# A four-block transformer kernel: the feed-forward with constants made earlier, statistics in three pieces, a new order of steps, and sums moved to TensorE

## The chip, the cores and the metric

The program runs on one core of a Trainium2 chip. A core has five engines that run their own instruction streams and meet at semaphores: TensorE (PE in the profile), VectorE (DVE), ScalarE (ACT), GpSimd (POOL) and SyncE (SP, which starts the transfers here). The metric is the device time of one execution in microseconds (us); lower is better.

## The reference, cut to what matters

The input x has 16 sequences of 256 tokens with 128 features. Four blocks follow each other, each as x + block(layernorm(x)): attention A (16 heads of 64, causal), the feed-forward, attention B (16 heads of 8), and the same feed-forward again. The change is in the feed-forward:

```python
h = gelu(concat(x, slot_mean) @ w1 + b1)
route_logits = (h @ w2 + b2) / (abs(tau) + 0.1)          # 64 slots per token
topk_vals, topk_idx = top_k(route_logits, 8)
alpha = (one_hot(topk_idx, 64) * softmax(topk_vals)[..., None]).sum(axis=-2)
si = einsum('bts,btd->bsd', alpha, x) / (alpha.sum(axis=1) + 1e-08)[..., None]
gi = si @ Wih.T + bih;  gh = S @ Whh.T + bhh             # S: the slots, the same for all
r = sigmoid(i_r + h_r);  z = sigmoid(i_z + h_z);  n = tanh(i_n + r * h_n)
S_new = (1.0 - z) * n + z * S
q = S_new @ wq + bq;  k = S_new @ wk + bk;  v = S_new @ wv + bv
y = S_new + softmax(q k^T * scale) @ v
y = (y - mean(y)) * rsqrt(var(y) + 1e-05) * ln_g + ln_b
out = einsum('bts,bsd->btd', alpha, y @ wvp + bvp) @ wo + bo
```

## The kernel before, in words

The residual X stays on chip as 32 tiles of 128 tokens by 128 features. The four blocks follow one another on every engine. Each block is written once per engine as a function `do` that says what this engine does in a step of a given kind; lists of steps (A_PLAN, B_PLAN, F_PLAN) give the order, the same list for all engines. An engine takes its steps strictly in that order and waits at semaphores (`f["..."]`, `a_...`, `b_...`), so a step late in the list can't start before an earlier one of the same engine.

*Attention A* works on one sequence and a group of four heads at a time; its last steps are in the last call of a_steps (lines 68 to 97) and in A_EPILOGUE (line 142), the drain: the last weighted sums (`pv`), their division (`normal`, DVE writes a_o), the transposes (`turn`), the projection (`project`: 16 products of 128 columns) and the addition to X on DVE. *Attention B* runs two sequences per trip; its drain is B_EPILOGUE (line 149). There POOL multiplies (line 891), DVE reduces (`gather`, line 858), POOL divides, the result goes through memory and back, PE transposes and projects it (`finish`, line 763), and ACT writes X.

*The feed-forward* treats the 32 tiles as two chunks of 16 (c = 0, 1). Its steps by name:
- `stats` and `apply`: the mean and variance of each token (bn_stats, bn_aggr on DVE), 1/sqrt by a power on POOL (norm_rstd, line 371), and the normalised tile f_xs on DVE (norm_apply, line 375). Chunk 0 has them as ffn_stats and ffn_apply in the drain of the attention ahead (lines 98 and 99, and B_EPILOGUE).
- `hidden`, `logits`: transposes of f_xs, a product with w1 and Gelu on ACT, a product with w2 (lines 917 to 939).
- `top`: DVE's max8 of 64 logits, the difference to the largest, and match_replace, which marks the eight taken (lines 1083 to 1096). `alpha`: exp on ACT, then on DVE the masked exp, its sum over 64, the reciprocal and the product (lines 1097 to 1104).
- `read`: PE sums the tokens of each slot and transposes alpha; ACT copies the transposes. `slots`, `inputs`: DVE divides (f_si, line 1115), PE transposes, ACT copies f_sit, PE multiplies by wih in three products of 512 columns (line 957).
- `gates`, `candidate`, `new`: DVE adds gate_h to two of them (line 1121), ACT's tanh, and the new slots f_sn. `qkv`, `scores`, `probs`, `attend`: the small attention among slots.
- `ynorm`: DVE subtracts y's mean and multiplies by 1/sqrt, PE transposes. `values`: the product with wcomb (ln_g, wvp and wo in one) and the addition of crow. `out`: 16 products with alpha, and DVE's addition to X in four pieces.

The order is `hidden`, `apply`, `logits` for both chunks, then `top 0`, `alpha 0`, `read 0`, `top 1`, `slots 0` and so on; from `gates` on, chunk 1 runs two steps behind chunk 0. gate_h, wcomb, crow and the other constants come from set_tensor and set_vector (lines 1200 to 1240), which run between attention A and the first feed-forward.

PSUM has eight banks. Each chunk of the feed-forward uses four (f_banks); the first transposes take banks 0 and 1, which attention A's projection also uses, so `hidden` 0 waits until all of X has been added.

## Time and profile before

| | |
|---|---|
| median of 3 runs | 945.12 us (944.6 to 946.56) |
| the profiled execution | 945.51 us, its span 943.7 us |
| mean granted TensorE clock | 0.922 |
| busy | PE 84%, DVE 71%, ACT 51%, POOL 43% of the span |
| attention A | to about 518 us |
| first feed-forward, with its constants | to about 615 us |
| attention B | to about 837 us |
| second feed-forward, with B's drain | to the end |

Times in the trace count from the span's start. A line of the timeline gives the start, the time from it to the end of the last instruction that it merges, the engine, the line of the kernel, the operation, what it writes and reads, and how many instructions; in brackets how long the engine had been idle and what ended that. The granted clock is a share of TensorE's full 2.4 GHz; it takes two levels, 0.5 and 1, so a value between is a mean over time.

### The profile page before, as it was taken

How to read it: one execution, taken by the hardware profiler on the slowest of the kernel's cores; microseconds unless marked ns; L12 is line 12 of the kernel's file. 1: busy time of each engine (PE TensorE's matmuls, PEld its weight loads, DVE VectorE, ACT ScalarE, POOL GpSimd, SP SyncE). 2: the span in 40 equal slices, each digit the busy share in tenths (PEclk: the TensorE clock that was granted, in tenths of full speed). 3: DMA queues.
4: the chain of work that ended last, by engine and by line, in shares of the span. 5: the costliest groups of instructions: out<-in, count | busy, mean ns of one | idle time of the engine just before them, and what ended most of it. 6: DMA issues, size and time to landing. Idle time of an engine off the chain costs nothing.

```text
span 943.7 us, 25617 instructions
## 1 busy us (share of the span) xinstructions
PE 789.8 (84%) x10324; PEld 606.5 (64%) x10324; DVE 672.3 (71%) x1528; ACT 480.2 (51%) x849; POOL 409.8 (43%) x302
## 2 busy tenths in 40 slices
PE   1899999999999999999986876667888888839655
PEld 0688888888888888888875553534555555525435
DVE  3767667776677766677674776536999999966773
ACT  1678766787767777677752423013444433315220
POOL 1454444544445444454442100116888888751000
PEclk9999999999999999999996778768999999958786
DMA  6000000000000000000000000000221111120002
GB/s 274 1 3 1 0 0 0 0 0 0 0 0 0 0 0 0 0 0 0 1 1 2 0 1 1 1 0 1 23 24 22 22 22 22 20 27 1 1 1 89
DMA packets 71588, 13.25 MB, mean 14 GB/s; under 512 B 66432, under 2 KB 70528, under 8 KB 70912
## 3 DMA queue, kind: packets, MB, share of 16 engines
q1 hardware_dynamic: 71552, 12.76, 6.2%
q8 instruction: 24, 0.39, 0.2%
q14 instruction: 12, 0.10, 0.0%
HBM read 8.56 MB, written 4.19 MB: 14 GB/s over the span
## 4 chain that ended last, share of the span: by engine, by line
PE 63%; DVE 19%; ACT 8%; issue 5%; POOL 3%; DMA 1%; DVEq 0%; ACTq 0%; SPq 0%; POOLq 0%
PE PS L533 6%; PE PS L490 6%; PE PS L349 5%; PE PS L350 4%; PE PS L351 4%; PE PS L426 3%; PE PS L732 3%; DVE b_prod L843 3%; PE PS L722 3%; PE PS L526 2%; PE PS L512 2%; PE PS L724 2%; PE PS L1015 2%; DVE a_nm L607 2%; PE PS L497 2%
## 5 line engine op out<-in xcount | busy, mean ns | idle before, releaser
L640 POOL TENSOR_TENSOR a_pl<-a_p,a_ph 128x1024 f16<-128x1024 f32 (+1 forms) x128 | 210.7, 1646 | 256.3 <-ACT a_ph L562 256.3
L891 POOL TENSOR_TENSOR b_w<-b_v,b_e 128x2048 f32<-128x2048 f32 x32 | 137.8, 4307 | 13.9 <-ACT b_e L811 13.9
L559 ACT ACTIVATE a_p<-PS 128x1024 f32<-128x1024 f32 (+1 forms) x128 | 103.7, 810 | 74.8 <-PE PS L497 74.7
L607 DVE TENSOR_REDUCE a_nm<-PS 128x4 bf16<-128x512 f32 (+1 forms) x128 | 121.5, 949 | 0.0
L843 DVE TENSOR_TENSOR b_prod<-PS,b_qt 128x512 f32<-128x512 f32 x128 | 85.4, 682 | 26.3 <-PE PS L724 22.0
L562 ACT ACTIVATE a_ph<-PS 128x1024 f16<-128x1024 f32 (+1 forms) x128 | 103.1, 805 | 0.0
L552 ACT ACTIVATE a_qk_h<-PS 128x512 f16<-128x512 f32 x128 | 73.4, 604 | 57.1 <-PE PS L351 55.8
L372 POOL TENSOR_TENSOR veps<-mv,eps 128x2 f32<-128x2 f32 (+2 forms) x40 | 8.0, 201 | 190.4 <-DVE mv L1165 136.9
L596 DVE TENSOR_TENSOR a_qk_l<-PS,a_qk_h 128x512 f16<-128x512 f32 x128 | 87.0, 681 | 3.4 <-ACT a_qk_h L552 3.4
L512 PE MATMUL PS<-a_vh,a_ph 128*128 128x65 f16 x768 | 78.5, 196 | 0.3 <-issue 0.3
L514 PE MATMUL PS<-a_vl,a_ph 128*128 128x64 f16 x768 | 78.3, 194 | 0.0
L516 PE MATMUL PS<-a_vh,a_pl 128*128 128x65 f16 x768 | 78.0, 195 | 0.0
L349 PE MATMUL PS<-xhl,a_wqk_h 128*128 128x256 f16 x256 | 70.8, 277 | 8.5 <-ACT xhl L550 7.5
L512 PEld LDWEIGHTS PS<-a_vh,a_ph 128*128 128x128 f16 x768 | 70.5, 98 | 11.1 <-issue 9.5
L858 DVE TENSOR_REDUCE b_s<-b_w 128x128 f32<-128x2048 f32 x32 | 72.8, 2277 | 4.9 <-POOL b_w L891 4.9
L722 PE MATMUL PS<-b_kh,w_rolls 128*128 128x256 f16 x256 | 65.9, 285 | 11.4 <-DVE b_prod L843 8.0
L603 DVE TENSOR_TENSOR a_vl<-PS,a_vh 128x512 f16<-128x512 f32 x64 | 44.3, 692 | 41.8 <-ACT a_vh L555 41.8
L514 PEld LDWEIGHTS PS<-a_vl,a_ph 128*128 128x128 f16 x768 | 71.4, 100 | 0.1
L516 PEld LDWEIGHTS PS<-a_vh,a_pl 128*128 128x128 f16 x768 | 71.4, 98 | 0.0
L351 PE MATMUL PS<-xhl,a_wqk_l 128*128 128x256 f16 x256 | 70.4, 275 | 0.0
L350 PE MATMUL PS<-xhl,a_wqk_h 128*128 128x256 f16 x256 | 70.3, 275 | 0.0
L724 PE MATMUL PS<-b_kl,w_rolls 128*128 128x256 f16 x256 | 65.3, 283 | 0.0
(225 smaller groups left out, 2038.7 us busy)
## 6 DMA issues: line engine op xcount, KB each, us to landing
scratch_dram<-b_o SPq DMA_DIRECT2D x32, 64.0 KB, 3.6
b_y<-scratch_dram SPq DMA_DIRECT2D x16, 128.0 KB, 2.1
out_dram<-X SPq DMA_DIRECT2D x2, 1024.0 KB, 3.9
w_rest<-rest_dram SPq DMA_DIRECT2D x1, 1862.0 KB, 15.2
X<-x_dram SPq DMA_DIRECT2D x1, 1792.0 KB, 11.2
w_first<-first_dram SPq DMA_DIRECT2D x1, 1600.0 KB, 7.1
w_rolls<-rolls_dram SPq DMA_DIRECT2D x1, 544.0 KB, 15.8
X<-x_dram SPq DMA_DIRECT2D x1, 256.0 KB, 3.6
```

The costliest lines, as they stand in the source:

```text
L349: pe.matmul(dst, ah, bh, start=start, stop=False, skip_group_check=True)
L350: pe.matmul(dst, ah, bl, start=False, stop=False, skip_group_check=True)
L351: return pe.matmul(dst, al, bh, start=False, stop=stop, skip_group_check=True)
L512: pe.matmul(O[q][:, h * W:(h + 1) * W], ph[:, nx, par, pair, at], a_vh[:, (g - 1) % GA, k, h, :], start=first, stop=False, skip_group_chec ...
L514: pe.matmul(O[q][:, h * W:h * W + EA], ph[:, nx, par, pair, at], a_vl[:, (g - 1) % GA, k, h, :], start=False, stop=False, skip_group_check ...
L516: ins = pe.matmul(O[q][:, h * W:(h + 1) * W], pl[:, nx, par, pair, at], a_vh[:, (g - 1) % GA, k, h, :], start=False, stop=h == 3 and k == ...
L559: act.activation((a_p0, a_p1)[j][:, me, :, :, :].rearrange("p a h q -> p a (h q)"), TT[:, :, 0:512 - 256 * j], ACT.Exp, scale=EA ** -0.5)
L562: act.activation((a_ph0, a_ph1)[j][:, me, :, :, :].rearrange("p a h q -> p a (h q)"), TT[:, :, 0:512 - 256 * j], ACT.Exp, scale=EA ** -0.5 ...
L607: dve.tensor_reduce(a_nm[:, nx, j, :].rearrange("p (a h) -> p a h", a=2)[:, :, 0:2], MM[:, :, 0:256 * (j + 1)].rearrange("p a (h k) -> p a ...
L640: pool.tensor_tensor(*(n[:, g % 2, :, :, :].rearrange("p a h q -> p (a h q)") for n in (pl, p, ph)), ALU.subtract).then_inc(a_split, 1)
L843: dve.tensor_tensor(b_prod[:, j, :, :], T[j % 2][:, :].rearrange("p (e t) -> p e t", e=2), b_qt[:, 1 - par, :].unsqueeze(1).to_broadcast([ ...
L891: pool.tensor_tensor(b_w8[:, j, :, :, :], rolled_values(par, j, 0, H), rolled_exps(par, j, 0, H), ALU.mult).then_inc(b_weighed, 1)
```

## The change: what it does

1. *Constants in the drain of A.* set_tensor and set_vector are split in two parts. Part 0 stands at the end of the last group of heads, ahead of ffn_apply; part 1 in A_EPILOGUE behind the last `normal`. All their sums now lie in two banks, S1 and S2.
2. *Statistics in three pieces* (PIECES): tiles 0 to 15, 16 to 27, 28 to 31. In the drain of A the second piece goes ahead of the last projection; in B the first piece moves into the last trip, ahead of a `gather`, and the second into B_EPILOGUE. Only four tiles are left for the feed-forward itself. `hidden` 0 uses banks 2 to 5 and no longer waits for the last addition to X; `hidden` 1 does.
3. *New order of steps* (F_PLAN). `top` is split into topa (max, differences) and topb (match_replace); topa of both chunks comes ahead of alpha 0. The exps are a step of their own. `add` is split from `out`.
4. *Gates and biases by TensorE.* PE starts the sums of the gates with a product of the identity and gate_h, and tanh reads them where they are; v starts with a product of ones and bv, and ACT copies it out.
5. *The softmax sum over 8 values*: the eight largest get their own differences and exps behind the 64, and DVE sums those.
6. *Centred weights.* wcomb has each column's mean over the rows taken off, so that y's mean drops out of the product. PE makes the transpose of y itself (identity by slots, v by p transposed), right behind y, and DVE multiplies by 1/sqrt when it adds crow. `ynorm` is gone.

```diff
-        put(last and g == 2, ("ffn_stats", 0))
-        put(last and g == 3, ("ffn_apply", 0))
+        put(last and g == 2, ("ffn_stats", 0), ("ffn_rstd", 0))
+        put(last and g == 3, ("set", 0), ("ffn_apply", 0))
...
     put(True, "sumexp")
+    put(tail, ("ffn_stats", 0))
...
-A_EPILOGUE = [("normal", 0, 0), ("turn", 0, 0), ("pv", 0, 0), ("pv", 0, 1), ("normal", 1, 0), ("turn", 1, 0),
-              ("project", 1, 0)]
+A_EPILOGUE = [("normal", 0, 0), ("turn", 0, 0), ("pv", 0, 0), ("pv", 0, 1), ("normal", 1, 0), ("set", 1, 1), ("turn", 1, 0),
+              ("ffn_stats", 1, 1), ("ffn_rstd", 1, 1), ("project", 1, 0)]
...
-              ("project", 1, 0), ("finish", 1, 0), ("ffn_stats", 0, 0), ("add", 1, 0), ("ffn_apply", 0, 0), ("yt", 1, 0),
+              ("ffn_rstd", 0, 0), ("ffn_stats", 0, 1), ("ffn_rstd", 0, 1), ("project", 1, 0), ("finish", 1, 0),
+              ("add", 1, 0), ("ffn_apply", 0, 0), ("yt", 1, 0),
...
+F_PLAN = [("stats", 2), ("hidden", 0), ("apply", 1), ("apply", 2), ("logits", 0), ("hidden", 1), ("logits", 1),
+          ("topa", 0), ("topb", 0), ("topa", 1), ("expo", 0), ("expo", 1), ("alpha", 0), ("read", 0), ("topb", 1), ("slots", 0),
+          ("inputs", 0), ("wih", 0), ("alpha", 1), ("gates", 0), ("candidate", 0), ("read", 1), ("new", 0), ("slots", 1),
+          ("qkv", 0), ("inputs", 1), ("scores", 0), ("wih", 1), ("gates", 1), ("probs", 0), ("candidate", 1), ("attend", 0),
+          ("new", 1), ("qkv", 1), ("values", 0), ("scores", 1), ("out", 0), ("probs", 1), ("attend", 1), ("add", 0),
+          ("values", 1), ("out", 1), ("add", 1)]
+PIECES = [(0, CT), (CT, CT - 4), (NT - 4, 4)]
...
                 if kind == "hidden":
-                    pe.wait_ge(f["normed"], k)
                     if c == 0:
+                        pe.wait_ge(f["normed"], len(PIECES) * rep + 1)
...
+                    else:
+                        pe.wait_ge(f["normed"], len(PIECES) * rep + 2)
                         pe.wait_ge((a_added, b_added)[rep], NB)
...
+                elif kind == "wih":
+                    pe.wait_ge(f["alt_ev"], k)
+                    for n in range(2):
+                        pe.matmul(B[2 + n][:, :].rearrange("p (b s) -> p b s", s=NS), ident[:, :],
+                                  gate_h[:, n:n + 1, :].to_broadcast([128, CB, NS]), start=True, stop=False)
                     pe.wait_ge(f["sit"], k)
...
                 elif kind == "qkv":
+                    pe.wait_ge(f["gates_tanh"], 2 * k)
+                    pe.matmul(B[2][:, :].rearrange("p (a d) -> p a d", a=PAIRS), ones[0:1, :],
+                              w["bv"].unsqueeze(1).to_broadcast([1, PAIRS, D]), start=True, stop=False, skip_group_check=True)
...
-                elif kind == "ynorm":
-                    pe.wait_ge(f["y"], k)
+                    pe.matmul(B[2][:, :], ident[:, :], v["sn"][:, :], start=True, stop=False, skip_group_check=True)
                     for p in range(PAIRS):
-                        ins = pe.transpose(B[2][:, p * 128:(p + 1) * 128], v["y"][:, p, :], ident[:, :])
+                        sl = slice(p * 128, (p + 1) * 128)
+                        ins = pe.matmul(B[2][:, sl], v["v"][:, p, :], v["pt"][:, sl], start=False, stop=p == PAIRS - 1,
+                                        skip_group_check=True)
                     ins.then_inc(f["yt_mm"], 1)
...
-                    link(dve.scalar_tensor_tensor(v["al"][:, :, :], f_z[:, :, :], TAKEN, f_e[:, :, :],
+                    link(dve.tensor_reduce(f_sum[:, :], v["e"][:, :, NS:NS + TOPK], X_AXIS, ALU.add))
+                    dve.reciprocal(f_sum[:, :], f_sum[:, :])
+                    link(dve.scalar_tensor_tensor(v["al"][:, :, :], f_z[:, :, :], TAKEN, v["e"][:, :, 0:NS],
                                                   ALU.is_equal, ALU.mult))
-                    link(dve.tensor_reduce(f_sum[:, :], v["al"][:, :, :], X_AXIS, ALU.add))
-                    link(dve.reciprocal(f_sum[:, :], f_sum[:, :]))
...
+                        ins = dve.scalar_tensor_tensor(v["so"][:, p, :], pairs(B[3][:, :])[:, p, :], rstd[:, n:n + 1],
+                                                       crow[:, :], ALU.mult, ALU.add)
...
+                dve.scalar_tensor_tensor(wcomb[:, :], S2[:, 256:384], -1.0 / D, wsum[:, :], ALU.mult, ALU.add)
```

The first place is VectorE in the drain of attention A, from the last a_nm but one division on. Before:

```order
L617 TENSOR_TENSOR a_o<-PS,a_rs 128x512
L377 TENSOR_SCALAR f_xs<-X,mv,rstd 128x128 x16
L616 RECIPROCAL a_rs<-PS 128x8
L617 TENSOR_TENSOR a_o<-PS,a_rs 128x512
L616 RECIPROCAL a_rs<-PS 128x8
L617 TENSOR_TENSOR a_o<-PS,a_rs 128x512
L623 TENSOR_TENSOR X<-PS,X 128x256
L1218 TENSOR_TENSOR brz<-w_rest 128x2
L1221 TENSOR_SCALAR gate_h<-PS,brz 128x64 x2
```

And now:

```order
L631 TENSOR_TENSOR a_o<-PS,a_rs 128x512
L1249 TENSOR_TENSOR brz<-w_rest 128x2
L1252 TENSOR_SCALAR gate_h<-PS,brz 128x64 x2
L1253 TENSOR_SCALAR hn_half<-PS,w_rest 128x64
L1254 TENSOR_SCALAR slot_mean<-PS 128x1
L1255 TENSOR_SCALAR cmid_rows<-ones,PS,w_rest 128x128
L1256 TENSOR_SCALAR wsum<-PS,w_rest 128x128
L379 TENSOR_SCALAR f_xs<-X,mv,rstd 128x128 x16
L630 RECIPROCAL a_rs<-PS 128x8
L631 TENSOR_TENSOR a_o<-PS,a_rs 128x512
L630 RECIPROCAL a_rs<-PS 128x8
```

The constants stand ahead of f_xs and, further on, ahead of the statistics of 12 tiles.

The second place is VectorE in the routing of the first feed-forward (f_v: the maxima, f_e: the exps, f_z: the logits with the taken ones marked, f_al: alpha). Before:

```order
L1087 MAX f_v<-PS 128x8 x16
L1090 TENSOR_TENSOR f_e<-PS,f_v 128x512 x2
L1094 MATCH_REPLACE f_z<-f_v,PS 128x64 x16
L1099 SCALAR_TENSOR_TENSOR f_al<-f_z,f_e 128x1024
L1101 TENSOR_REDUCE f_sum<-f_al 128x16
L1102 RECIPROCAL f_sum<-f_sum 128x16
L1103 TENSOR_TENSOR f_al<-f_al,f_sum 128x1024
L1087 MAX f_v<-PS 128x8 x16
L1090 TENSOR_TENSOR f_e<-PS,f_v 128x512 x2
L1094 MATCH_REPLACE f_z<-f_v,PS 128x64 x16
L1109 TENSOR_SCALAR f_den<-PS 128x2 x2
```

And now:

```order
L1122 MAX f_v<-PS 128x8 x16
L1124 TENSOR_TENSOR f_e<-f_v 128x16x8
L1127 TENSOR_TENSOR f_e<-PS,f_v 128x8x64 x2
L1132 MATCH_REPLACE f_z<-f_v,PS 128x64 x16
L1122 MAX f_v<-PS 128x8 x16
L1124 TENSOR_TENSOR f_e<-f_v 128x16x8
L1127 TENSOR_TENSOR f_e<-PS,f_v 128x8x64 x2
L1137 TENSOR_REDUCE f_sum<-f_e 128x16
L1138 RECIPROCAL f_sum<-f_sum 128x16
L1139 SCALAR_TENSOR_TENSOR f_al<-f_z,f_e 128x1024
L1141 TENSOR_TENSOR f_al<-f_al,f_sum 128x1024
L1132 MATCH_REPLACE f_z<-f_v,PS 128x64 x16
```

The maxima and differences of chunk 1 stand ahead of the first f_al, and its MATCH_REPLACE behind it.

The third place is TensorE from the end of chunk 0's read to its scores. Before:

```order
L952 MATMUL PS<-w_first,f_si 128x128 x4
L957 MATMUL PS<-f_sit,w_rest 128x512 x3
L941 MATMUL PS<-f_xs,f_al 64x129 x16
L946 MATMUL PS<-w_first,f_al 128x128 x8
L952 MATMUL PS<-w_first,f_si 128x128 x4
L957 MATMUL PS<-f_sit,w_rest 128x512 x3
L962 MATMUL PS<-f_sn,w_rest 64x512
L964 MATMUL PS<-w_rest,f_sn 128x128 x4
L973 MATMUL PS<-f_k,f_q 64x64 x8
```

And now:

```order
L978 MATMUL PS<-w_first,f_si 128x128 x4
L983 MATMUL PS<-gate_h,w_first 128x512 x2
L987 MATMUL PS<-f_sit,w_rest 128x512 x3
L967 MATMUL PS<-f_xs,f_al 64x129 x16
L972 MATMUL PS<-w_first,f_al 128x128 x8
L991 MATMUL PS<-w_rest,ones 128x512
L994 MATMUL PS<-f_sn,w_rest 64x512
L996 MATMUL PS<-w_rest,f_sn 128x128 x4
L978 MATMUL PS<-w_first,f_si 128x128 x4
L1005 MATMUL PS<-f_k,f_q 64x64 x8
L983 MATMUL PS<-gate_h,w_first 128x512 x2
L987 MATMUL PS<-f_sit,w_rest 128x512 x3
```

The two products of gate_h stand ahead of those of f_sit, the bias of v (ones by w_rest) ahead of f_sn, and chunk 1's slot sums and transposes come between.

## Rows read from the trace of the kernel before

**Rows 1.** The page's chain that ended last: shares of the span by engine.

```profile
PE 63%; DVE 19%; ACT 8%; issue 5%; POOL 3%; DMA 1%; DVEq 0%; ACTq 0%; SPq 0%; POOLq 0%
```

**Rows 2.** Windows, first feed-forward: length, each engine's busy time, clock, DMA share, GB/s.

```profile
core 0: us, PE busy (x) PEld busy (x) DVE busy (x) ACT busy (x) POOL busy (x), PEclk, DMA share, GB/s
518.31:615.13 96.82, 68.93 (x412) 47.40 (x410) 63.79 (x251) 25.88 (x40) 5.55 (x6) 0.77 0.00 1
```

**Rows 3.** Timeline, drain of attention A: start, length, engine, line, operation.

```profile
498.97 2.12 POOL L640 TENSOR_TENSOR a_pl<-a_p,a_ph 128x1024 f16<-128x1024 f32 x1
499.04 6.82 DVE L377 TENSOR_SCALAR f_xs<-X,mv,rstd 128x128 f32<-128x128 f32 x16 [2.31 <-POOL rstd L373]
...
499.96 0.28 PE L497 MATMUL PS<-a_nmt,w_masks 64*128 64x128 bf16 x4
...
518.31 0.42 DVE L623 TENSOR_TENSOR X<-PS,X 128x256 f32<-128x256 f32 x1 [7.44 <-PE PS L533]
```

**Rows 4.** Timeline, the constants and the first transposes of the feed-forward.

```profile
518.11 0.78 PE L1204 MATMUL PS<-w_rest 128*128 128x64 f32 x6
...
520.46 0.48 DVE L1221 TENSOR_SCALAR gate_h<-PS,brz 128x64 f32<-128x64 f32 x2 [1.52 <-PE PS L1209]
...
521.36 0.29 DVE L1225 COPY bv_rows<-PS 128x128 f32<-128x128 f32 x1
521.56 0.34 DVE L1226 TENSOR_SCALAR wcomb<-PS,w_rest 128x128 f32<-128x128 f32 x1
...
522.59 0.48 PE L1213 MATMUL PS<-w_rest,ones 1*128 1x128 f32 x2
...
524.21 1.97 PE L923 MATMUL PS<-w_first,f_xs 128*128 128x128 f32 x8 [1.14 <-DVE crow L1239]
```

**Rows 5.** Timeline, the router and the routing in both feed-forwards.

```profile
532.88 3.79 PE L933 MATMUL PS<-w2s,f_h 65*128 65x64 f32 x32
...
536.50 1.75 PE L923 MATMUL PS<-w_first,f_xs 128*128 128x128 f32 x8
...
544.12 4.56 PE L933 MATMUL PS<-w2s,f_h 65*128 65x64 f32 x32
...
551.33 2.19 DVE L1087 MAX8 f_v<-PS 128x8 f32<-128x64 f32 x16
...
551.47 3.71 PE L941 MATMUL PS<-f_xs,f_al 128*64 128x129 f32 x32 [2.79 <-DVE f_al L1103]
553.56 1.29 DVE L1090 TENSOR_TENSOR f_e<-PS,f_v 128x512 f32<-128x512 f32 x2
...
868.65 3.79 PE L933 MATMUL PS<-w2s,f_h 65*128 65x64 f32 x32
```

**Rows 6.** Timeline, prices in the slot part and in the last output products.

```profile
560.04 0.60 ACT L1045 ACTIVATE f_sit<-PS 128x512 f32<-128x512 f32 x1 [1.84 <-PE PS L952]
...
571.40 2.84 PE L957 MATMUL PS<-f_sit,w_rest 128*128 128x512 f32 x6 [1.73 <-ACT f_sit L1045]
...
600.20 2.06 PE L1007 MATMUL PS<-f_so,f_alt 64*128 64x128 f32 x32
...
609.98 3.79 PE L1007 MATMUL PS<-f_so,f_alt 64*128 64x128 f32 x32 [0.78 <-DVE f_so L1176]
...
613.81 1.29 DVE L1184 TENSOR_TENSOR X<-PS,X 128x512 f32<-128x512 f32 x2 [0.42 <-PE PS L1007]
```

**Rows 7.** Timeline, drain of attention B.

```profile
829.95 2.29 DVE L858 TENSOR_REDUCE b_s<-b_w 128x128 f32<-128x2048 f32 x1 [2.31 <-POOL b_w L891]
...
834.78 2.29 DVE L858 TENSOR_REDUCE b_s<-b_w 128x128 f32<-128x2048 f32 x1 [2.55 <-POOL b_w L891]
...
844.70 4.19 DVE L377 TENSOR_SCALAR f_xs<-X,mv,rstd 128x128 f32<-128x128 f32 x16 [3.33 <-POOL rstd L373]
...
846.66 1.06 PE L763 MATMUL PS<-w_rest,b_yt 128*128 128x128 f32 x4
```

**Rows 8.** Windows, the slot part from slots 0 to the end, and its middle.

```profile
559.29:615.10 55.81, 35.71 (x240) 25.25 (x240) 32.87 (x73) 11.22 (x19) 2.42 (x4) 0.79 0.00 1
...
565.00:579.00 14.00, 9.50 (x77) 5.78 (x76) 9.87 (x19) 5.05 (x9) 0.00 (x0) 1.00 0.00 1
```

More of the change, by code:

```diff
@@ L167 @@
           (b_steps(0) + b_steps(1), 2, NB // 2 - 3),
-          (b_steps(0, ahead2=False) + b_steps(1, ahead=False, ahead2=False), NB // 2 - 1, None),
+          (b_steps(0, ahead2=False) + b_steps(1, ahead=False, ahead2=False, tail=True), NB // 2 - 1, None),
           (B_EPILOGUE, NB // 2, None)]
-F_PLAN = [("stats", 1), ("hidden", 0), ("apply", 1), ("logits", 0), ("hidden", 1),
-          ("logits", 1), ("top", 0), ("alpha", 0), ("read", 0), ("top", 1), ("slots", 0), ("inputs", 0), ("alpha", 1),
-          ("read", 1), ("gates", 0), ("slots", 1), ("inputs", 1)]
-LATER = ["gates", "candidate", "new", "qkv", "scores", "probs", "attend", "ynorm", "values", "out"]
-F_PLAN.append(("candidate", 0))
-for n in range(2, len(LATER) + 2):
-    F_PLAN += [(LATER[m], c) for m, c in ((n, 0), (n - 2, 1)) if m < len(LATER)]
+F_PLAN = [("stats", 2), ("hidden", 0), ("apply", 1), ("apply", 2), ("logits", 0), ("hidden", 1), ("logits", 1),
[5 more added lines that the diff above has]
+PIECES = [(0, CT), (CT, CT - 4), (NT - 4, 4)]
 class Fill:
@@ L631, in do @@
                 u = GA * b + g
[L632 to L633 removed]
+                if kind == "ffn_rstd":
+                    rstd_piece(pool, chain.link, 0, j)
                 elif kind == "norm":
@@ L1046, in do @@
                 elif kind == "gates":
-                    act.wait_ge(f["gates"], k)
-                    act.activation(v["r"][:, :], v["r"][:, :], ACT.Tanh, scale=0.5)
-                    act.activation(v["zg"][:, :], v["zg"][:, :], ACT.Tanh, scale=0.5).then_inc(f["gates_tanh"], 1)
+                    for n, dst in ((0, v["r"]), (1, v["zg"])):
+                        act.wait_ge(f["gi_mm"], 3 * (k - 1) + n + 1)
+                        act.activation(dst[:, :], B[2 + n][:, :], ACT.Tanh, scale=0.5).then_inc(f["gates_tanh"], 1)
                 elif kind == "candidate":
@@ L1055, in do @@
                     act.activation(v["q"][:, :], B[0][0:DQ, :], ACT.Identity, bias=w["bqk"][0:DQ, :]).then_inc(f["q"], 1)
+                    act.wait_ge(f["v_mm"], k)
+                    act.activation(v["v"][:, :, :].rearrange("p a d -> p (a d)"), B[2][:, :], ACT.Copy).then_inc(f["v"], 1)
                 elif kind == "scores":
@@ new lines, in build, with set_tensor @@
+        S1, S2 = PS[4], PS[5]
+        def set_tensor(pe, part):
+            if part == 0:
+                pe.wait_ge(w_loaded, 16 * 2)
+                for n in range(3):
+                    pe.matmul(S1[:, n * NS:(n + 1) * NS], w["whh_t"][:, n * 128:(n + 1) * 128], w["slot_t"],
+                              start=True, stop=True)
+                pe.matmul(S1[:, 192:193], w["slot"], ones[0:NS, 0:1], start=True, stop=True)
+                pe.matmul(S1[:, 193:194], w["wvp"], w["ln_b"], start=True, stop=True)
+                pe.matmul(S1[:, 256:384], w["wvp_t"], w["wo"], start=True, stop=True).then_inc(set_mm, 1)
+            else:
+                pe.wait_ge(set_ev, 1)
+                pe.matmul(S2[0:DH, 0:1], w["w1b"], slot_mean[:, :], start=True, stop=True)
+                pe.matmul(S2[:, 128:256], cmid_rows[:, :], w["wo"], start=True, stop=False)
+                pe.matmul(S2[:, 128:256], ones[0:1, :], w["bo"], start=False, stop=True)
+                pe.matmul(S2[:, 256:384], ones[:, :], wsum[:, :], start=True, stop=True).then_inc(set_mm, 1)
@@ new lines, in set_vector @@
+        def set_vector(dve, link, part):
+            if part == 0:
+                dve.wait_ge(w_loaded, 16 * 2)
+                link(dve.tensor_tensor(brz[:, :], w["bih"][:, 0:2], w["bhh"][:, 0:2], ALU.add))
+                dve.wait_ge(set_mm, 1)
+                for n in range(2):
+                    dve.tensor_scalar(gate_h[:, n, :], S1[:, n * NS:(n + 1) * NS], brz[:, n:n + 1], None, ALU.add)
+                dve.tensor_scalar(hn_half[:, :], S1[:, 2 * NS:3 * NS], w["bhh"][:, 2:3], 0.5, ALU.add, ALU.mult)
+                dve.tensor_scalar(slot_mean[:, :], S1[:, 192:193], 1.0 / NS, None, ALU.mult)
+                dve.tensor_scalar(cmid_rows[:, :], ones[:, :], S1[:, 193:194], w["bvp"], ALU.mult, ALU.add)
+                dve.tensor_scalar(wsum[:, :], S1[:, 256:384], w["ln_g"], None, ALU.mult).then_inc(set_ev, 1)
+            else:
+                link(dve.scalar_tensor_tensor(inv_tau[:, 0:1], w["tau"], -1.0, w["tau"], ALU.mult, ALU.max))
+                link(dve.tensor_scalar(inv_tau[:, 0:1], inv_tau[:, 0:1], 0.1, None, ALU.add))
+                link(dve.reciprocal(inv_tau[:, 1:2], inv_tau[:, 0:1]))
+                dve.tensor_scalar(w2s[:, :], w["w2b"], inv_tau[:, 1:2], None, ALU.mult)
+                dve.memset(ones_h[:, :], 1.0)
+                dve.tensor_copy(b_bo_h[:, :], w["b_bo"])
+                link(dve.tensor_copy(b_w_h[:, :, :], w["b_wqkv"]))
+                dve.tensor_tensor(b_bo_l[:, :], w["b_bo"], b_bo_h[:, :], ALU.subtract)
+                dve.tensor_tensor(b_w_l[:, :, :], w["b_wqkv"], b_w_h[:, :, :], ALU.subtract)
+                dve.wait_ge(set_mm, 2)
+                dve.tensor_tensor(c1[:, :], S2[0:DH, 0:1], w["b1"], ALU.add)
+                dve.scalar_tensor_tensor(wcomb[:, :], S2[:, 256:384], -1.0 / D, wsum[:, :], ALU.mult, ALU.add)
+                dve.tensor_copy(crow[:, :], S2[:, 128:256]).then_inc(consts_set, 1)
```

181 lines of the change are left out of this document (75 added, 106 removed).

## The prediction

> **What bounds the kernel now.** I read the page's chain first [rows 1]: PE holds 63% of it, DVE 19%, and no transfer matters. Then I asked for the window of the first feed-forward [rows 2]: 96.8 us, PE busy 71% of it and DVE 66%, at a mean granted clock of 0.77; the second reads alike. No engine is full there; each waits for another in turn, and TensorE is partly at 1.2 GHz. Between the feed-forwards nothing changes but one step at each end, so the time must come from four places: the drain of attention A, the routing, the slot part, the drain of attention B. I walk each in the timeline, and write "to" for a span in microseconds of the trace before.
>
> **Drain of A and the constants.** Before, project ends just ahead of its addition at 518.31 [rows 3], then PE and DVE hand each other the constants until 524.2, when the first transposes of f_xs start [rows 4]. The change cuts this out of the end and puts it ahead of two things that are themselves on the path.
> - Part 0 on PE follows the last score product, which ends at 500.2 [rows 3]. Its products took 518.1 to 520.3 with the bias row, 1.8 without it, so they end at 502.1. DVE then evicts for 1.2 (520.46 to 521.90, without the copy of bv_rows, 0.2) [rows 4]: f_xs starts at 503.3 and not at 499.04.
> - But f_xs then runs alone. Before it took 6.82 while POOL was on a_pl; the same 16 took 4.19 in the drain of B [rows 3, 7]. At 4.2 it ends at 507.5 and a_o, queued behind it, moves by +1.6.
> - Part 1 on PE stands between the weighted sums and turn. Three products took 1.1 (521.96 to 523.07) [rows 4], four at the half clock about 2.2; some of it lies beside DVE's a_o. I take +0.8, bounds 0 and +2.2.
> - Project then ends at 520.7, and the transposes follow at once: 520.7 for 524.2, **-3.5**. DVE has 7.44 of idle before project's addition [rows 3], which covers its part 1 (about 3) and the statistics of 12 tiles (about 3.2): nothing. The last piece, 4 tiles, and the applies of 16 end near 527, ahead of hidden 1.
> - PE now goes from project into hidden without a gap. Hidden 0 took 8.7 (524.21 to 532.88) behind PE's pause, hidden 1, straight behind logits 0, took 7.6 (536.50 to 544.12) [rows 4, 5]. I take most of the difference: **-0.7**, bounds 0 and -1.1.
>
> A rule bears on the second point. The Trainium skill (SBUF — State Buffer, "SBUF: two separate sides") says that GpSimd and a two-port VectorE operation take their shared pair of ports by an exclusive lock, and the loser blocks for the whole instruction. By that rule f_xs takes 4.2 here. If something else stretched it before, it stays at 6.82 and the sum is 2.6 higher.
>
> **Drain of B.** Before, DVE did statistics (4.4, from 837.0 to 841.4), waited 3.33 for POOL's power, and normalised 4.19 until 848.9 [rows 7]. Now the first statistics go before DVE's next to last reduction. DVE sat idle for 2.31 before that one and 2.55 before the last [rows 7]: 4.4 of statistics from 827.7 end at 832.1, the reduction of 2.3 at 834.4, before POOL releases the last at 834.8. So nothing is lost, and by 0.4 only. The power (3.3) runs from 838, f_xs ends near 845.3, even with 2.4 of stretching by 847.7. Then PE's finish of the last pair sets the start: it ends at 847.7, for 848.9 [rows 7]: **-1.2**.
>
> **Routing (both feed-forwards).** The order now puts chunk 1's maxima ahead of chunk 0's alpha. From the first transposes to the end of logits 1 is 24.5 (524.2 to 548.7) [rows 4, 5]. After that come max (2.2), two subtractions (1.2) and one on 128 elements (0.2), and then alpha in 3.0 in place of 4.0, since the sum runs over 8 values and not 64. Alpha 0 ends after 31.1, where it ended after 27.2 (read started on it at 551.47) [rows 5]. This is a loss of 3.9. It comes back: before, DVE did all of top 1 ahead of slots 0, which ended at 559.3 [rows 8], 7.9 after alpha 0. Now only match_replace is left of it (7.9, less slots' own 1.2, less 2.2 and 1.2: 3.3), beside read's 3.7 on PE [rows 5], and slots 0 ends 5.0 after. Net +1.0 in the first, +0.2 in the second, whose logits 1 ended 23.5 after its first transposes (872.4 less 848.9) [rows 5, 7]: **+1.2**.
>
> **Slot part (both).** From the end of slots 0 to the last addition took 55.8, with PE busy 35.7 of it [rows 8]. On DVE the change removes four gate additions, two v additions (ACT copies v instead) and the eight y normalisations; so becomes four instructions a chunk where it was one, 1.4 for 0.7. On PE it adds, per chunk, four products of 512 columns (two gates, bias of v, slots in transposed y) and puts products where the four transposes of y stood. With centred weights the mean needs no subtraction, so yt is made beside the statistics and no longer behind them. Prices at 2.4 GHz: 0.85 for 512 columns (2.84 for three) or four times 128, ACT's copy 0.6, DVE's 0.65 for 512 elements [rows 6]. Walked in PE's new order, times from the end of slots 0:
> 1. Alt transposes, two copies of ACT, sit: 1.9, then five products 4.3: 6.2. Read 1 and alt 2.9, bias 0.9: 10.0; new 0 is just ready.
> 2. qk, v, si 1, scores 0: 3.1; gates of chunk 1 4.3; transposes of p and ACT's copy 1.3: 18.7.
> 3. Attend 0 with yt 3.5, bias 0.9, a wait of 0.9 for new 1 (DVE takes y's statistics first), qk, v, values 0, scores 1 3.6: 27.6.
> 4. DVE's so 1.0 more, out 0 2.0, probs 1 another 0.8, its transposes and copy 1.3, attend 1 3.5: 36.2.
> 5. Copy, values 1 1.7; DVE's add 0 and so 1.7: 39.6. Out 1 and the last additions 2.8 at 2.4 GHz: 42.4.
>
> Before, the last out ran at the half clock, 3.79 for 2.06 [rows 6]. I assume that again for this step alone: 39.6 + 3.8 + 1.3 + 0.1 = 44.8, or -11.0, twice: **-22.0**. Bounds: 42.4, and 50 if the clock is no better than before (next part).
>
> **Sum.** -3.5 - 0.7 - 1.2 + 1.2 - 22.0 = -26.2. From the profiled execution's 945.5 that is 919.3; the median shown is 0.4 lower, so 918.9, given as **919**. Two tenths of a per cent, 1.9 us, is about what a measurement of this kernel can tell from no change.
>
> **Rivals.**
> - *The clock does not improve.* In the slot part the mean clock was 0.79 [rows 8], where 0.5 is 1.2 GHz and 1 is 2.4: that is 42% of the time, and some 27% of the work, at 1.2 GHz. The same share on 33 us of path work costs 0.27 x 33 x 0.85 = 7.6 over 42.4: 50.0, and the kernel takes 919 + 2 x 5.2 = 929. For it: long hand-overs stay (attend, probs, so). Against: PE's long waits for p, for y's normalisation and for the gates become waits of about 1. The Trainium skill (TensorE: Matmul & The Clock Gate, "What's actually happening") says that "the default state is throttled, and activity releases the throttle", which speaks for the forecast. Chance 15%.
> - *More than forecast*: all at 2.4 GHz, 919 - 2 x 2.4 - 1 = 913 or less. 4%.
> - *Slower: TensorE becomes the bound at 1.2 GHz.* PE has eight more 512-column products per feed-forward, 1.7 each at that clock. If it falls there and stays, the path's 33 us become 61 and the slot part 71: 919 + 2 x 26.2 = 971. It decides from 44.8 + 13.1 = 57.9 on, which is 55% of the path work at 1.2 GHz. The first rows after an idle stretch did run so: out at 3.79 [rows 6], read at 3.71 [rows 5]. Against it: from 565 to 579, where PE was busy 68% of the time, the granted clock was 1.00 [rows 8], and the new order is denser than that. 5%.
> - *The reordering only shifts the wait*: DVE, behind chunk 1's maxima and y's statistics, lets PE wait where the gate additions stood, and the two effects cancel. That needs 11 us of new waits per feed-forward, of which I find none over 1. 2%.
>
> **Numbers.** The forecast holds 74% (914 to 926), the clock rival 15%, more gain 4%, slower 5%, cancelled 2%. The range 913 to 931 takes in the bounds of the slot part (42.4 and 50) and of the drain (+2.6, +1.4), and leaves out under 2 in 10. Faster by over 0.2%: 0.93; within: 0.02; slower: 0.05.
>
> **What would show it.** f_xs in the first drain should take about 4.2 from 503; the first transposes of f_xs come under 0.2 after project; the last reductions of B stay at 832 and 834.8 relative to the loop. Alpha 0 should end 31 after the transposes, slots 0 36. From there to the last addition 42 to 47, with a clock of 0.85 or more. I am wrong if that stretch is over 50, if PE waits over 2 us for new or so, or if the statistics in B push the last reduction.

## The result and the profile after

The changed kernel takes **911.06 us** (median of 3, 910.95 to 911.65) for 945.12: ratio 0.9638, 95% interval 0.9616 to 0.966. The forecast was 919 with a range of 913 to 931, so the direction was right and the gain of 34 larger than the range allows. The profiled execution has a span of 909.3 us for 943.7, at a mean granted clock of 0.957 for 0.922.

Windows of the changed kernel, cut at the borders that the prediction used (first transposes of f_xs, end of logits 1, end of slots 0, last addition); columns: window, length, busy time of PE, PEld, DVE, ACT and POOL, granted clock, DMA share, GB/s:

```profile
497.20:522.40 25.20, 17.64 (x161) 15.73 (x158) 13.33 (x65) 4.81 (x7) 8.60 (x5) 0.67 0.01 2
522.40:542.52 20.12, 19.55 (x114) 12.17 (x112) 12.61 (x77) 13.21 (x19) 1.25 (x2) 1.00 0.00 1
542.52:554.27 11.75, 5.06 (x39) 4.73 (x40) 10.78 (x61) 1.17 (x1) 0.00 (x0) 0.59 0.00 0
554.27:597.90 43.63, 35.99 (x267) 24.28 (x265) 26.22 (x65) 12.64 (x22) 3.21 (x4) 0.99 0.00 1
597.90:625.00 27.10, 16.61 (x103) 8.75 (x104) 8.49 (x25) 8.15 (x21) 4.68 (x13) 0.72 0.00 1
...
828.39:849.61 21.22, 20.96 (x113) 13.06 (x112) 12.19 (x76) 13.84 (x20) 1.25 (x2) 0.93 0.00 0
849.61:861.35 11.74, 5.05 (x39) 4.72 (x40) 10.77 (x61) 1.16 (x1) 0.00 (x0) 0.60 0.01 2
861.35:904.97 43.62, 36.05 (x267) 24.34 (x265) 26.21 (x66) 12.64 (x22) 3.21 (x4) 0.99 0.06 25
```

The same cuts in the kernel before, the slot part being in [rows 8]:

```profile
524.20:548.70 24.50, 24.47 (x112) 14.87 (x112) 16.36 (x101) 13.58 (x19) 3.13 (x2) 0.78 0.00 1
548.70:559.29 10.59, 5.61 (x40) 4.88 (x40) 10.38 (x58) 1.09 (x2) 0.00 (x0) 0.60 0.00 0
...
615.10:642.20 27.10, 16.79 (x95) 8.21 (x95) 8.11 (x24) 6.58 (x18) 3.72 (x12) 0.63 0.00 0
...
848.95:872.40 23.45, 23.45 (x112) 14.36 (x112) 15.56 (x100) 13.59 (x19) 3.13 (x2) 0.82 0.00 1
```

The two routers, 522.40 to 542.52 and 524.20 to 548.70, are the rows to read. PE was busy nearly all through both, 19.55 of 20.12 us and 24.47 of 24.50, on 114 and 112 records of the same work. What differs is the granted clock, 1.00 for 0.78, and with it 4.4 us. The slot part falls from 55.8 to 43.6 though PE is busy 0.3 us longer. Its clock goes from 0.79 to 0.99.

| stretch | before | forecast | after |
|---|---|---|---|
| first transposes of f_xs, start | 524.2 | 520.7 | 522.4 |
| router 0 | 24.5 | 23.8 | 20.1 |
| end of logits 1 to slots 0 | 10.6 | 11.6 | 11.75 |
| slot part, each | 55.8 / 55.6 | 44.8 | 43.6 |
| end of the first feed-forward to the last reduction of B | 219.7 | 219.7 | 217.7 |
| from there to the transposes | 14.2 | 13.0 | 12.75 |
| router 1 | 23.5 | 23.5 | 21.2 |

### The profile page after: what moved, and what is told of

It is laid out like the page before. It is cut to its first block, busy times and chain, and to the rows that moved or that the text cites. A ratio compares the mean times of both kernels' runs of the same rounds, so it can differ in the third digit from the quotient of the medians.

```text
span 909.3 us, 25722 instructions
## 1 busy us (share of the span) xinstructions
PE 782.6 (86%) x10372; PEld 602.1 (66%) x10372; DVE 654.3 (72%) x1518; ACT 482.3 (53%) x853; POOL 412.1 (45%) x306
## 3 DMA queue, kind: packets, MB, share of 16 engines
HBM read 8.56 MB, written 4.19 MB: 14 GB/s over the span
## 4 chain that ended last, share of the span: by engine, by line
PE 68%; DVE 15%; ACT 7%; issue 5%; POOL 2%; DMA 1%; DVEq 0%; SPq 0%; ACTq 0%; POOLq 0%
PE PS L543 7%; PE PS L500 6%; PE PS L351 5%; PE PS L352 4%; PE PS L353 4%; PE PS L432 4%; DVE b_prod L857 3%; PE PS L746 3%; PE PS L736 3%; PE PS L536 3%; PE PS L522 3%; PE PS L738 2%; PE PS L507 2%; PE PS L526 2%; DVE a_nm L621 2%
## 5 line engine op out<-in xcount | busy, mean ns | idle before, releaser
L857 DVE TENSOR_TENSOR b_prod<-PS,b_qt 128x512 f32<-128x512 f32 x128 | 85.1, 681 | 24.6 <-PE PS L738 20.2
L374 POOL TENSOR_TENSOR veps<-mv,eps 128x2 f32<-128x2 f32 (+3 forms) x42 | 9.1, 215 | 166.3 <-DVE mv L1196 126.9
L736 PE MATMUL PS<-b_kh,w_rolls 128*128 128x256 f16 x256 | 64.8, 282 | 11.6 <-DVE b_prod L857 8.1
```

The lines of the kernel that those rows point to most:

```text
L857: dve.tensor_tensor(b_prod[:, j, :, :], T[j % 2][:, :].rearrange("p (e t) -> p e t", e=2), b_qt[:, 1 - par, :].unsqueeze(1).to_broadcast([ ...
```

## The experiments

All of these do the whole computation; "idle products" are products into a bank that nobody reads, added and not taken from anything. The one that says `again` is the changed kernel itself. Times of slot parts are from the end of slots 0 to the end of the last addition, first and second feed-forward.

**consts_late**: the constants made after attention A again.

```diff
-        put(last and g == 3, ("set", 0), ("ffn_apply", 0))
+        put(last and g == 3, ("ffn_apply", 0))
...
-A_EPILOGUE = [..., ("normal", 1, 0), ("set", 1, 1), ("turn", 1, 0),
+A_EPILOGUE = [..., ("normal", 1, 0), ("turn", 1, 0),
...
             a_tensor(pe)
+            set_tensor(pe, 0)
+            set_tensor(pe, 1)
```

> The changed kernel with its constants made behind attention A again, between its last projection and the first transposes of f_xs; statistics in pieces, order and slot part stay. Clock theory (a pause of TensorE at the entry costs its clock for several us behind the pause): the first transposes start about 3 us later, and the first router, from first transposes to the end of logits 1, goes back from 20.1 us at a granted clock of 1.00 to about 24.5 at 0.78; 911.1 + 3 + 4.4 = 918.5. Rival (the router became faster for the order of its statistics and its banks alone): only the 3 us of the drain return, the router stays at 20.1, 914. The second feed-forward stays as it is in both.

Measured 916.63 us, ratio 0.969 (0.9671 to 0.9709). Its windows, from the first transposes:

```profile
523.38:547.90 24.52, 24.48 (x112) 14.63 (x112) 12.05 (x76) 13.77 (x19) 1.25 (x2) 0.78 0.00 1
...
559.63:603.25 43.62, 35.95 (x267) 24.23 (x265) 26.21 (x65) 12.64 (x22) 3.21 (x4) 0.99 0.00 1
```

The router is back at 24.5 us and 0.78, within 0.02 us of what it was before, with the statistics and banks as changed. The transposes came only 1.0 later than in the profile of the changed kernel, not 3, but that profile had lost 1.4 us long before the drain: its last a_o but two is done at 497.81, here at 496.40. From there to the transposes it is 27.0 us here and 24.6 in the changed kernel (24.4 in `again`). So moving the constants was worth 2.4 in the drain and 4.4 in the router behind it: the larger part of the gain lies where nothing was edited. The times agree with the profile: the four executions here take 915.1 to 918.0, the eight of the changed kernel 909.4 to 911.7 but for one.

**order_old**: the new operations, steps in the old order.

```diff
-F_PLAN = [..., ("topa", 1), ("expo", 0), ("expo", 1), ("alpha", 0), ("read", 0), ("topb", 1), ("slots", 0), ...
+F_PLAN = [..., ("expo", 0), ("alpha", 0), ("read", 0), ("topa", 1), ("topb", 1), ("expo", 1), ("slots", 0), ...
+LATER = ["gates", "candidate", "new", "qkv", "scores", "probs", "attend", "values", "out", "add"]
+F_PLAN.append(("candidate", 0))
+for n in range(2, len(LATER) + 2):
+    F_PLAN += [(LATER[m], c) for m, c in ((n, 0), (n - 2, 1)) if m < len(LATER)]
```

> The changed kernel with the old order of the steps in both feed-forwards, with its new operations (gates by TensorE, centred weights) kept. If the order is what fills TensorE's waits and so holds its clock: the slot part goes from 43.6 us to 50 or so with a clock under 0.9 and the last out back at 3.8 us instead of 2.06, twice, about 922. Rival (the operations taken from DVE carry the gain, the order only shifts waits): 911 within 2 us.

Measured 936.23, ratio 0.9891 (0.9862 to 0.9921). The slot parts took 55.8 and 57.5, no better than before the change although DVE is busy 6.5 less in each. (The profile is of one of its two longer executions, 938.46; the four lie between 933.8 and 938.7.) TensorE waits for p again, the transposes behind take 1.12 and not 0.6, and both outs run at the half clock, 3.79 and 3.67:

```profile
580.23 1.12 PE L1012 MATMUL PS<-w_first,f_p 128*128 128x128 f32 x4 [4.94 <-DVE f_p L1187]
...
595.22 1.12 PE L1012 MATMUL PS<-w_first,f_p 128*128 128x128 f32 x4 [2.73 <-DVE f_p L1187]
596.27 3.79 PE L1041 MATMUL PS<-f_so,f_alt 64*128 64x128 f32 x32
```

**before_warm**: the kernel before, with idle products.

```diff
+        def warm(pe, bank, n):
+            for _ in range(n):
+                pe.matmul(bank[:, :], ident[:, :], <w["wih_t"], 512 columns>, start=True, stop=True)
...
                 elif kind == "probs":
+                    if c == 0:
+                        warm(pe, B[0], 5)
                     pe.wait_ge(f["prob"], k)
...
                 elif kind == "ynorm":
+                    warm(pe, B[2], 3)
                     pe.wait_ge(f["y"], k)
```

> The kernel before, unchanged but for idle products of 512 columns into a bank that is free: 5 ahead of TensorE's wait for p of chunk 0, and 3 ahead of each wait for the normalised y. Nothing else is removed. Clock theory: out of chunk 1 falls from 3.79 to 2.06 us, the transposes of y and values of chunk 1 from 1.11 + 2.07 to about 0.6 + 1.06, and the start of attention B gains the 1.9 us that it gained in the change: 945.1 - 2 x 3.2 - 1.9 = 937. Rival (the time is set by the chain of dependent steps and the clock is no part of it): 945 within 1, or slower by what the idle products delay.

Measured **934.01**, ratio 0.9874 (0.9857 to 0.9892). A kernel that only does more takes 11 us less. Slot parts 51.2 and 50.2, clocks 0.91 and 0.97. The first of the two outs that the expectation speaks of, and the idle products ahead of it:

```profile
599.78 2.85 PE L913 MATMUL PS<-w_rest,w_first 128*128 128x512 f32 x6
602.91 0.66 PE L1000 MATMUL PS<-w_first,f_y 128*128 128x128 f32 x4 [0.28 <-DVE f_y L1179]
604.25 1.16 PE L1006 MATMUL PS<-wcomb,f_yt 128*128 128x128 f32 x8 [0.69 <-ACT f_yt L1072]
606.20 2.06 PE L1015 MATMUL PS<-f_so,f_alt 64*128 64x128 f32 x32 [0.78 <-DVE f_so L1184]
```

These are the products that took 1.11, 2.07 and 3.79 before (the last is in [rows 6]):

```profile
605.32 1.11 PE L992 MATMUL PS<-w_first,f_y 128*128 128x128 f32 x4 [3.06 <-DVE f_y L1171]
607.12 2.07 PE L998 MATMUL PS<-wcomb,f_yt 128*128 128x128 f32 x8 [0.69 <-ACT f_yt L1064]
```

I had expected 937; the clock is worth about 5 in each slot part, not 3.2.

**order_warm**: order_old with 5 and 3 idle products ahead of the waits for p.

> The changed kernel with the old order, and with 5 and 3 idle products ahead of TensorE's waits for p. The run with the old order took 936.2, its slot parts 55.8 and 57.5 at a clock of 0.79 and 0.77. If the order's worth is mostly the clock: slot parts near 46, 936 - 22 = 914. If it is mostly the waits themselves (4.9 and 2.7 for p, 3.0 for the first si): the clock returns 5 in each, as the same products gave in the kernel before, 926.

Measured 925.48, ratio 0.9789 (0.9773 to 0.9806); slot parts 51.3 and 51.5. The clock returns 4.5 and 6.0, much as in before_warm. The other 8 come only with the order. I read most of them as waits that it fills, but this is not shown: the last outs here still took 3.60 and 3.67.

**ops_old**: the new order, with gates, v and y by DVE again.

```diff
-                        pe.matmul(B[2 + n][:, :]..., ident[:, :], gate_h[:, n:n + 1, :].to_broadcast(...), start=True, stop=False)
+                        dve.tensor_tensor(slots(dst[:, :]), slots(B[2 + n][:, :]), gate_h[...], ALU.add)
...
-                    act.activation(v["v"]..., B[2][:, :], ACT.Copy).then_inc(f["v"], 1)
+                    dve.tensor_tensor(v["v"][:, :, :], pairs(B[2][:, :]), bv_rows[...], ALU.add).then_inc(f["v"], 1)
...
-                        ins = pe.matmul(B[2][:, sl], v["v"][:, p, :], v["pt"][:, sl], start=False, ...)
+                        ins = dve.tensor_scalar(v["y"][:, p, :], ..., mv[:, n, 0:1], rstd[:, n:n + 1], ALU.subtract, ALU.mult)
+                        ins = pe.transpose(B[2][:, p * 128:(p + 1) * 128], v["y"][:, p, :], ident[:, :])
```

> The changed kernel with its new order, but with the old operations of the slot part: gate additions, v's addition and the normalising of y by DVE, y turned behind it by TensorE. With the old order and the new operations the slot part took 55.8 us, as before, so I ask whether the order carries the gain alone. If it does: slot part 44 to 46, the kernel 912 to 916. If order and operations need each other: the operations put 6.6 us more on DVE in each slot part and a wait for the normalised y (3.1 to 3.6 before) back on TensorE, with the clock lost behind it: slot part about 51, the kernel 926.

Measured 936.73, ratio 0.9921 (0.9886 to 0.9956); slot parts 55.6 and 55.7. In these profiles neither the order alone (here) nor the operations alone (order_old) gains anything in the slot part; together they gain 12.2.

**y_dve**: of these, only y undone.

> The changed kernel with one thing undone: y normalised by DVE and then turned by TensorE, as before; gates and v stay as changed. If y's chain (statistics, power, normalising, transposes, copy, values) is what TensorE waits for in the new order too: per chunk 1.9 of power and normalising and 0.7 of the copy come ahead of values, less 1.9 of products that fall away; the last chunk has no cover, so the slot part is 3 longer and the last out falls to the half clock, 3.8 for 2.06: 911 + 2 x 4.5 = 920. Rival (qk and v of chunk 1 and out of chunk 0 cover it): 911 to 913.

Measured 935.53, ratio 0.9874 (0.9844 to 0.9905), above both expectations; slot parts 52.6 and 52.9. My undo had a flaw: y of chunk 1 stood behind the four additions of chunk 0 on DVE. Two runs put it ahead of them (a step "ynorm" before ("add", 0)).

**ops_old2** and **y_dve2**: ops_old and y_dve with y of chunk 1 ahead of the additions.

> The run with the new order and the old operations (936.7), with one step of DVE moved: y of chunk 1 is normalised ahead of the additions of chunk 0 (2.45 us) and no longer behind them. In the run before, TensorE waited 5.04 us for that y, and its last transposes, values and out ran at the half clock. If the queue on DVE was the cause: the wait falls to 2.6, the slot part from 55.6 to about 52 (a little more if the clock holds), the kernel to 929. If the old operations cost by themselves, as my reading is: 55.6 goes to 53 at best and stays 9 over the changed kernel's 43.6.

> The changed kernel with y alone normalised by DVE and turned by TensorE, and this time with y of chunk 1 ahead of the additions of chunk 0 on DVE. The first such run took 935.5 with slot parts of 52.6 and 52.9. If the queue behind the additions (2.45 us) made that cost: slot part about 46, the kernel 917. If y's chain itself does, with the clock behind its wait: 51 or more, the kernel 929 to 932.

Measured 930.26, ratio 0.9821 (0.9805 to 0.9838), slot parts 54.8 and 55.2; and 929.47, ratio 0.9833 (0.9805 to 0.9861), slot parts 52.1 and 52.0. The flaw cost 0.5 to 1.0 in a slot part; of the 6 us between y_dve and y_dve2, 2.9 are the first router (23.1 for 20.1) and 1.4 lie ahead of it. Y's chain itself costs 8.4 to 8.5 in each slot part. What gates and v add is less clear: with them undone besides, the median is 0.8 higher, but the slot parts are 2.7 and 3.3 longer, in a profile of ops_old2's longest execution (934.88; the others took 928.9 to 930.6). The end of the first slot part in y_dve2, then in the changed kernel:

```profile
596.78 1.11 PE L1024 MATMUL PS<-w_first,f_y 128*128 128x128 f32 x4 [4.16 <-DVE f_y L1200]
598.58 2.07 PE L1029 MATMUL PS<-wcomb,f_yt 128*128 128x128 f32 x8 [0.69 <-ACT f_yt L1100]
601.44 3.79 PE L1038 MATMUL PS<-f_so,f_alt 64*128 64x128 f32 x32 [0.78 <-DVE f_so L1205]
```

```profile
590.02 1.05 PE L1024 MATMUL PS<-f_pt,f_v 128*128 128x128 f32 x8
591.76 1.16 PE L1031 MATMUL PS<-wcomb,f_yt 128*128 128x128 f32 x8 [0.69 <-ACT f_yt L1102]
594.21 2.06 PE L1040 MATMUL PS<-f_so,f_alt 64*128 64x128 f32 x32 [1.29 <-DVE f_so L1203]
```

The wait of 4.16 is gone, the one for yt (0.69) stays, the one for so grows from 0.78 to 1.29; and the three steps take 4.3 in place of 7.0.

**ops_warm**: ops_old2 with idle products ahead of qkv (1 and 3) and of y (2 and 5).

> As the run ops_old2, and with idle products ahead of TensorE's waits: 1 and 3 ahead of qkv of chunks 0 and 1, 2 and 5 ahead of the normalised y. Tells how much of what old operations cost under the new order is the clock. If it is mostly the clock: slot part 46 to 47, the kernel 917. If it is half: 49 to 50, 923. If it is the waits alone: as ops_old2, or slower by what the products delay.

Measured 921.34, ratio 0.9732 (0.9716 to 0.9749); slot parts 48.3 and 47.9. Of the 11.2 and 11.6 that separate ops_old2 from the changed kernel, the idle products give back 6.5 and 7.4.

**gates_dve**: only the gates' additions undone.

> The changed kernel with one thing undone: the gates' additions by DVE again (two of 0.65 us a chunk), four products of 0.85 us less on TensorE in a feed-forward. Theory (TensorE's waits set the slot part, and its clock with them): the tanh of each chunk comes 1.3 later, and TensorE has 1.7 less to do while it waits for new: waits of 2 to 3 us ahead of qk of both chunks, a half clock behind them, slot part 43.6 + 1.3 + 1.3 + 2 = 48, the kernel 920. Rival (DVE has room and TensorE has less to do): slot part 43 to 45, 911 to 914.

Measured 912.42, ratio 0.9642 (0.9625 to 0.966); slot parts 42.1 and 42.6. My theory was wrong here: TensorE found no wait over 1.4 us to fall into, and the slot parts are 1.0 to 1.6 shorter. The kernel is no faster for it, since in this profile the first router took 23.0 (below). Gates by TensorE gain nothing in the changed kernel.

**alpha_first**: alpha 0 ahead of the maxima of chunk 1.

```diff
-          ("topa", 0), ("topb", 0), ("topa", 1), ("expo", 0), ("expo", 1), ("alpha", 0), ("read", 0), ("topb", 1), ("slots", 0),
+          ("topa", 0), ("topb", 0), ("expo", 0), ("alpha", 0), ("topa", 1), ("expo", 1), ("read", 0), ("slots", 0), ("topb", 1),
```

> The changed kernel with one row of its order moved: alpha of chunk 0 goes ahead of the maxima of chunk 1, and slots 0 ahead of the replacing of chunk 1. My reading of the routing: DVE sits idle for 3.12 us before the maxima of chunk 1, while the exponentials of chunk 0 end at 542.0; alpha 0 then ends at about 545 in place of 549.2, read 0 follows, and slots 0 ends about 4 us earlier, with DVE's work for chunk 1 beside TensorE's gates of chunk 0. About 4 us in each feed-forward: 903. Rival: alpha 1 and read 1 come later than TensorE wants them (DVE is the bound of this stretch), so that the slot part grows by most of what the routing saves: 909 to 911.

Measured **902.56**, ratio 0.9559 (0.9528 to 0.9591). Routing and slot part of the first feed-forward:

```profile
541.70:549.01 7.31, 4.49 (x41) 4.08 (x40) 7.17 (x29) 1.14 (x2) 0.00 (x0) 0.77 0.00 0
549.01:592.86 43.85, 35.66 (x264) 23.81 (x264) 29.39 (x96) 12.55 (x23) 3.22 (x4) 1.00 0.00 1
```

Slots 0 end 7.3 after logits 1 and not 11.75 (6.8 in the second feed-forward); the slot part pays 0.2 of it back.

**alpha_warm** and **alpha_warm2**: alpha_first with idle products in the long waits that are left.

> The run with alpha 0 ahead (902.6), and idle products in TensorE's long waits: 7 in the drain of A behind the first constants, 2 ahead of read 0, 5 behind the last out of the first feed-forward, 10 and 3 in the drain of B. Clock theory: part 1 of the constants and project run at 2.4 GHz (2), the reads (1.2 each), the start of B (3), the drain of B with hidden 0 (2.5): 902.6 - 9 = 893 to 895. Rival (the idle products stand in the way, or the records' clock is not what the waits cost): 902 or more.

> The run alpha_warm (896.2) with one more idle product, ahead of the wait for so of chunk 1 (1.29 us). In the profile of alpha_warm the last out of the first feed-forward took 3.68 and not 2.06. If the wait is what cost the clock there: 2.06 in both feed-forwards, 895 to 896. If the clock's fall depends on more than the last wait: no difference within 1.5 us.

Measured 896.25, ratio 0.9475 (0.9459 to 0.9491), and **896.20**, ratio 0.9469 (0.9453 to 0.9485). In alpha_warm the reads take 1.99; in alpha_warm2 the clock from 800 to the second transposes is 1.00, where the changed kernel had 0.69. The drain of A stays at 0.75 with PE busy 22.2 of 23.0 us, which I can't explain. One more product ahead of the last out made no difference in the median.

**best**: alpha_warm2 with the gates' additions on DVE, for the 1.2 us that gates_dve had shown.

> The run alpha_warm2 (896.2) with the gates' additions back on DVE. In the run gates_dve the slot parts took 42.1 and 42.6 us where the changed kernel's took 43.6. If that holds with alpha 0 ahead, 1.2 in each: 893.8. Rival (DVE is fuller in this order, its replacing of chunk 1 stands behind slots 0, so the additions come later): 896 to 898.

Measured 906.18 (902.76 to 913.0), ratio 0.9597 (0.9561 to 0.9633): wrong by ten, and on the other side. With alpha 0 ahead DVE is late with the gates: TensorE waits 1.58 for the new slots, where alpha_first had 0.19, and is at the half clock behind it:

```profile
557.39 1.82 PE L1003 MATMUL PS<-f_sn,w_rest 128*64 128x512 f32 x2 [1.58 <-DVE f_sn L1188]
559.14 2.03 PE L1005 MATMUL PS<-w_rest,f_sn 128*128 128x128 f32 x8
```

The same two steps took 1.07 and 1.16 in the changed kernel, and the slot parts are 48.5 and 46.8. What gates_dve says holds for its own order only. The best version found is alpha_warm2.

**again**: the changed kernel, five more executions.

> The changed kernel itself, for more executions of it. In the profiles of kernels whose work ahead of the first router is the same, that router took 20.1 us at a clock of 1.00 in some and 23.1 at 0.85 in others, with TensorE busy all through. If the phase of the clock against the work changes from one execution to the next: some executions lie 2 to 5 us over 911, as with other kernels here. If it belongs to the kernel: all within 0.8 us, as the first three (910.95 to 911.65).

Measured 909.43, 909.99, 910.81, 911.23 and 916.17, ratio 0.9635 (0.961 to 0.966). Four belong to the kernel, one lies 5 over at a mean clock of 0.942 for 0.953 to 0.957.

## Why the prediction was right and wrong

**Right.** The mechanism and most terms.
- In the drain of A f_xs started at 504.5 for 503.3 (503.0 in `again`) and took 4.18 for the 4.2 forecast. The last a_pl on POOL is over before it starts:

```profile
502.60 1.15 POOL L654 TENSOR_TENSOR a_pl<-a_p,a_ph 128x512 f16<-128x512 f32 x1 [0.42 <-ACT a_ph L572]
504.50 4.18 DVE L379 TENSOR_SCALAR f_xs<-X,mv,rstd 128x128 f32<-128x128 f32 x16
```

  Before, two of the sixteen took most of the extra time, 2.14 and 1.17 us, and ended within 0.1 of POOL's two a_pl (501.1 and 502.7); in consts_late, with a_pl beside them again, the sixteen took 6.83:

```profile
499.04 2.14 DVE L377 TENSOR_SCALAR f_xs<-X,mv,rstd 128x128 f32<-128x128 f32 x1 [2.31 <-POOL rstd L373]
...
501.61 1.17 DVE L377 TENSOR_SCALAR f_xs<-X,mv,rstd 128x128 f32<-128x128 f32 x1
```

  The exclusive lock of the Trainium skill (SBUF — State Buffer, "SBUF: two separate sides") says the same, that the loser blocks for the whole instruction, and for a_pl the trace agrees. Beside POOL's power it does not (last section).
- The drain of B: -1.4 for -1.2. The early statistics pushed neither reduction; the last still waited 0.73 for POOL. No run undoes the statistics in pieces, so that this gain is theirs is read from the timeline.
- Routing: logits 1 to slots 0 took 11.75 for 11.6. Alpha 0 ended 26.8 after the transposes and not 31, all of it the shorter router. That the loss in the routing was avoidable the forecast did not see: alpha_first takes 4.2 off the first feed-forward and 4.7 off the second.
- Slot part: 43.6 for 44.8.

**Wrong: the sum, by -8.** From 943.7 the span fell by 34.4 where the terms gave 26.2. Step by step:
- *"Hidden 0 took 8.7 behind PE's pause ... I take most of the difference: -0.7"* is the term that failed. Hidden 0 took 6.4, so it gained 2.3, past the bound of -1.1; and logits 0, hidden 1 and logits 1 stood in the sum as before the change, though hidden 1 gained 1.3 and logits 1 0.8. The reason lies in the measure that I took: hidden 1, which was to show the work without a pause, itself ran partly at the half clock (0.59 from 536 to 540, last section), and at 1.00 it takes 6.3 and not 7.6. The router took 20.1 and 21.2 for 23.8 and 23.5, another -3.7 and -2.3 beyond the forecast. consts_late shows the cause of the first: with the pause back it is 24.5 at 0.78. For the second no run shows a cause: in twelve profiles with the same work ahead of that router it took 20.9 to 22.1 in eleven and 24.4 in one (ops_warm).
- *"Before, the last out ran at the half clock. I assume that again for this step alone"*: it took 2.06. Twice -1.2 after what other steps gave back.
- The start of attention B had no term. It gained 1.9: the clock there is 0.72 for 0.63. The out at the full clock ahead of it is not the whole cause: every profile with an out of 2.06 has the short start, but so have order_old, ops_old and order_warm, whose outs took 3.67, 3.79 and 3.60.
- Against these, the transposes came at 522.4 and not 520.7. 1.1 of that lies at the start of attention A, where products of 256 columns still took 0.42 at 28.1 us (before, they took 0.27 from 24.8 on), nothing that was edited. It belongs to that execution and not to the kernel: in `again` they took 0.27 from 24.3 on, and the transposes start at 520.81, where the forecast had them. The drain itself, from the last a_o but two to the transposes, gave 2.9 (3.1 in `again`) of the 3.5. The rest is project (5.73 for 5.39) and part 1 of the constants (+1.2 for +0.8), partly at the half clock.
- Together 1.7 - 3.7 - 2.3 - 1.9 - 2.4 = -8.6, against the -8.2 found.

So the error is nearly all of one kind: the clock was priced in the one stretch where waits were removed, and there too low by the last out, and it was left as it was in three others. What raised it is shown for the slot parts and the first router, and stays open for the second router and the start of attention B. The rival "all at 2.4 GHz" came nearest and had 4%; I had put its gain at 6 us and counted little beside the slot parts. The Trainium skill's sentence (TensorE: Matmul & The Clock Gate, "What's actually happening": "the default state is throttled, and activity releases the throttle") speaks for this, and before_warm agrees in the plainest form: products that do nothing but keep TensorE active take 4.6 and 5.4 us off the slot parts.

**Right for a wrong reason: the size of the slot part.** The walk took DVE's removed instructions, TensorE's added ones and the order as terms that add up. They don't. In the profiles the order alone gives between -0.1 and 1.0 in a slot part (ops_old, ops_old2), the operations alone 0.0 and -1.9 (order_old), both together 12.2 and 12.0. Other executions of ops_old2 and order_old were up to 6.0 and 4.6 us shorter than the profiled ones; if all of that lay in the two slot parts, order and operations would still add up to some 6 of the 12.2. Of the operations y's path counts most (8.4 to 8.5, y_dve2) and the gates nothing (gates_dve); v was never undone alone. About half of the 12.2 is the clock: idle products give 4.5 to 7.4 in each of the three incomplete versions.

What stays open: why the drain of A stays slow in alpha_warm2, and when the clock falls in a stretch without gaps. The softmax sum over 8 values was not undone in any run either.
